# A state-space mixer's head: the second normalisation on ScalarE, and another order of the first step

## The chip, the cores and the metric

The kernel runs on one core of a Trainium2 chip. The metric is the device time of one execution in microseconds, the median of several runs. TensorE multiplies, VectorE, ScalarE and GpSimd compute element by element, SyncE (SP) issues most of the transfers; ScalarE's instruction stream issues some too. Each engine runs its own list of instructions strictly in order, and the engines wait for one another through counted semaphores.

## What is computed

Input x is 2 sequences of 2048 tokens with 256 features, float32. A conditioning vector c gives six modulation rows per sequence. Then:

```python
h = _layernorm(x) * (1 + ca) + sa
xn = _layernorm(h, ln_w, ln_b)          # the second normalisation
xz = xn @ W_in.T                        # xp and z, 512 channels each
xc = silu(conv1d(xp, 4 taps) + b_conv)
dt, B, C = split(xc @ W_x.T)            # 16 + 16 + 16 rows
dt = softplus(dt @ W_dt.T + b_dt)
h_t = h_{t-1} * exp(dt_t * A) + dt_t * u_t * B_t    # 16 states a channel
y = ((h_t . C_t) + xc * D) * silu(z)
# forward and backward over time, then x + ga * (h + 0.5 * (y_fwd + y_bwd) @ W_out.T)
# then a second modulated normalisation and a mixture of 8 experts, 2 taken per token, and a shared one
```

## The kernel before

The tokens are 8 blocks of 512. The kernel has a head, a scan stage and an expert stage; the change touches the head and the first units of the scan stage.

**The scan stage** has 16 steps q (block and direction alternating, even q forward). A step has 16 units T, four to each chunk c of 128 channels. A unit has 4 parts i. For a unit VectorE multiplies the step input by the B rows (`multiply`, L1350; every fourth unit GpSimd does it, L798), ScalarE computes four decays exp(dt*A) into the PSUM banks 0 to 3 (`decay`, L1102), VectorE scans the four parts (`scan`, L1364), GpSimd multiplies by the C rows (`weigh`, L810), and TensorE adds up the states of four units (`sum_chunk`, L1760 and L1764). A decay of part i waits until the part's previous scan has read the bank (`scan_done`), so ScalarE can be at most one unit ahead. TensorE brings 32 channels of the step input to all partitions (`spread_input(U)`, L1752); it needs VectorE's multiply two units earlier to be done, as there is one bank.

While a step is scanned, the engines prepare the next one in fixed slots (T mod 16, n): projections of xp (`project_x`, L1689), convolution as 4 tap matmuls (`convolve`, L1708), their copies by ScalarE (`copy_xp`, L1011 to 1018, `copy_conv`, L1045), silu (L1052), the 48 rows of B, C and dt (`project_xdbl`, L1731, `copy_x_dbl`, L1059), `project_dt` (L1740) and softplus in three passes (L1071, L1073, L1076) and a log (L1082). GpSimd adds the two parts of softplus (`add_dt`, L785) and multiplies dt by xc (`step_input`, L790). All of these share two PSUM banks in one fixed sequence (`bank_uses`). In the T loop ScalarE's slots CONV_AT are (2,1), (2,2), (5,1), (6,0): `copy_conv(q+1, 0)` comes after decay (2,1).

**Transfers of a step.** SP runs one list. `spread_rows(q)` stores the B and C rows and loads them to all partitions, 8 transfers of 256 KB (L577). `store_dt` (L585) writes a chunk's dt to DRAM, `spread_dt` (L594) reads it back broadcast (4 x 256 KB) for the decays, `spread_dtu` (L603, L608) does so with dt*xc for GpSimd's multiply. Everything SP issues goes into one queue.

**The head** prepares all 8 blocks in the order of ORDER. For each block n VectorE takes statistics of x (L1278, L1281, L1284), modulates (L1293, L1299) to H, takes statistics of H, and one block later normalises (`normalise`, L1310) into one of three buffers xn. GpSimd computes the reciprocal roots (`power`, L761) and, ahead of that, the diagonal tap matrices of both directions (L771, 8 instructions), which SP stores in DRAM and loads again where they are needed. TensorE turns a block (`turn_block`, L1665), ScalarE copies it with ln_w and ln_b applied (`copy_turned`, L980) and issues two stores (`keep_block`): H to t_scratch and the turned block to xnT_scratch, 512 KB each. Blocks 0 and 1 are also the first two steps' inputs. The first step's own preparation is woven between the blocks by hand, on TensorE and on ScalarE. At its end stand the last block's copy, behind decay (0,3), and before it the scaling of w_out (L1130). SBUF of the head lies under the buffers dbu and hst of the scan stage, so before the first multiply VectorE waits for the taps to be stored and for mod_scratch (`taps_kept`, `mod_stored`; SP issues the latter at L630, behind spread_dt(0, 0)), and before unit 2's scans for all H and xnT stores. The order of the blocks between the steps, and two of the waits:

```python
copy_block(3)
copy_x_dbl(0)
softplus(0, 0)
softplus_log(0, 0)
for c in range(1, NC):
    softplus(0, c)
softplus_log(0, 1)
copy_block(4)
...
dve.wait_ge(taps_kept, 32)
dve.wait_ge(mod_stored, 16)
multiply(0)
```

## Time and profile before

| | |
|---|---|
| median of 3 runs | 2238.55 us (2237.41 to 2240.18) |
| the profiled execution, its own time | 2238.26 us |
| its span in the profile | 2236.5 us |
| busy: PE, PEld, DVE, ACT, POOL | 83%, 34%, 92%, 60%, 81% |
| granted TensorE clock, mean | 0.874 |
| DMA, mean | 116 GB/s |

Times in rows are microseconds from the start of the span unless marked otherwise. PE is TensorE, PEld its weight loads, DVE VectorE, ACT ScalarE, POOL GpSimd; SPq and ACTq are the instructions by which those engines issue transfers. In a line of the timeline the first number is the start, the second the duration of the merged group, and a bracket tells how long the engine was idle before it and what ended that. A float32 matmul is recorded as two instructions. The clock column is a share of 2.4 GHz.

### The profile page before, as it was taken

To read this page: it belongs to the slowest core of one execution; us is meant where nothing else is said; L and a number is where in the kernel's file an instruction comes from. 1 tells how busy PE (TensorE), PEld (TensorE's weight loads), DVE (VectorE), ACT (ScalarE), POOL (GpSimd) and SP (SyncE) were. 2 spreads that over 40 slices of the span, in tenths; PEclk is the share of its full clock that TensorE was granted. 3 is DMA by queue.
4 is the path that set the end of the run, shared out by engine and by line. 5 is a ranking of instruction groups with operands and counts; after the bars stand their busy time and mean duration, and the time that the engine had idled before them with its cause. 6 is when DMAs were issued, how large, how long until landed. Compare 5 with 4: busy or idle time off the path is not lost.

```text
span 2236.5 us, 24275 instructions
## 1 busy us (share of the span) xinstructions
PE 1847.3 (83%) x6152; PEld 765.3 (34%) x6153; DVE 2047.3 (92%) x2381; ACT 1342.3 (60%) x2404; POOL 1811.6 (81%) x652
## 2 busy tenths in 40 slices
PE   7687887878797879788787878797956699999997
PEld 3222332323232323233232323231312366655554
DVE  7899999999999999999999999999999877557776
ACT  3566757585766757675758576666755343424443
POOL 3389999999999999999999999999999434325444
PEclk9777988989898979798898989797967799999999
DMA  7734434343434344353534353444434462235554
GB/s 285 227 89 106 121 102 123 96 112 106 113 106 112 107 115 115 100 121 101 125 94 115 103 120 105 105 109 119 96 89 134 161 237 102 83 86 83 79 80 67
DMA packets 136494, 259.95 MB, mean 116 GB/s; under 512 B 19984, under 2 KB 42768, under 8 KB 135232
## 3 DMA queue, kind: packets, MB, share of 16 engines
q1 hardware_dynamic: 120064, 230.78, 38.8%
q0 software_dynamic: 13440, 17.93, 4.8%
q10 hardware_dynamic: 2880, 9.96, 1.1%
q8 instruction: 46, 0.75, 0.1%
q14 instruction: 64, 0.52, 0.1%
HBM read 190.32 MB, written 69.34 MB: 116 GB/s over the span
## 4 chain that ended last, share of the span: by engine, by line
DVE 47%; PE 22%; issue 14%; POOL 5%; ACT 4%; DMA 3%; DVEq 3%; SPq 1%; POOLq 0%; ACTq 0%
DVE hst L1364 30%; DVE dbu L1350 9%; PE psum L1764 4%; PE psum L1889 4%; POOL hst L810 3%; PE psum L1708 3%; PE psum L1722 2%; PE psum L1901 2%; PE psum L1752 2%; DVEq L1598 1%; DVE h L1608 1%; PE psum L1689 1%; DVE h L1620 1%; DMA b_rep<-bc_scratch 1%; ACT psum L1102 1%
## 5 line engine op out<-in xcount | busy, mean ns | idle before, releaser
L810 POOL TENSOR_TENSOR hst<-hst,c_rep 128x2048 f32<-128x2048 f32 x255 | 1152.1, 4536 | 22.6 <-ACT state L1090 20.1
L1102 ACT ACTIVATE psum<-dt_rep,neg_a 128x512 f32<-128x512 f32 x1024 | 692.8, 684 | 442.8 <-DVE hst L1364 433.8
L1364 DVE TENSOR_TENSOR_SCAN hst<-psum,state,dbu 128x512 f32<-128x512 f32 x768 | 919.3, 1257 | 0.0
L1350 DVE TENSOR_TENSOR dbu<-psum,b_rep 128x2048 f32<-128x2048 f32 x192 | 434.8, 2265 | 17.3 <-PE psum L1752 12.8
L1752 PE MATMUL psum<-dt,same 32*128 32x512 f32 x384 | 253.0, 743 | 192.8 <-DVE dbu L1350 184.5
L1764 PE MATMUL psum<-hst,same 128*32 128x512 f32 x2048 | 311.4, 763 | 50.3 <-POOL hst L810 42.0
L798 POOL TENSOR_TENSOR dbu<-dtu_rep,b_rep 128x2048 f32<-128x2048 f32 x64 | 291.7, 4558 | 45.8 <-DVE hst L1364 45.8
L1364 DVE TENSOR_TENSOR_SCAN hst<-psum,dbu 128x512 f32<-128x512 f32 x256 | 291.1, 1198 | 0.7 <-ACT psum L1102 0.7
L1708 PE MATMUL psum<-xp,taps 128*128 128x512 f32 x512 | 246.6, 632 | 5.6 <-ACTq L1019 4.8
L930 POOL DMA_INDIRECT out_x<-h,target_u x72 | 113.2, 1572 | 156.9 <-DMA out_x<-h,target_u 77.5
L1752 PEld LDWEIGHTS psum<-dt,same 32*128 32x128 f32 x384 | 64.9, 208 | 339.6 <-DVE dbu L1350 255.7
L1764 PEld LDWEIGHTS psum<-hst,same 128*32 128x32 f32 x2048 | 71.9, 136 | 301.7 <-issue 222.3
L1952 PE MATMUL psum<-w,h 128*128 x288 | 145.0, 627 | 8.2 <-issue 2.8
L1708 PEld LDWEIGHTS psum<-xp,taps 128*128 128x128 f32 x512 | 98.8, 200 | 150.8 <-issue 149.7
L1689 PE MATMUL psum<-xnT,w_in 128*128 128x512 f32 x256 | 133.2, 647 | 18.4 <-ACT xc L1045 17.4
L894 POOL DMA_INDIRECT slot_scratch<-send,slot_u x64 | 64.4, 1006 | 102.4 <-ACT send L1202 79.4
L1696 PE MATMUL psum<-xnT,w_in 128*128 128x512 f32 x256 | 127.9, 625 | 11.5 <-ACT sz L1028 11.3
L1760 PE MATMUL psum<-xc,diag_d 128*128 128x512 f32 x128 | 96.0, 841 | 50.0 <-DVE sz L1343 50.0
L1722 PE MATMUL psum<-w_out,sz 128*128 128x256 f32 x512 | 117.0, 382 | 0.0
L1889 PE MATMUL psum<-h2T,sw 128*128 128x512 f32 x256 | 114.8, 602 | 0.4 <-ACT g_silu L1188 0.4
L1722 PEld LDWEIGHTS psum<-w_out,sz 128*128 128x128 f32 x512 | 98.3, 192 | 27.5 <-issue 15.6
L1602 DVE TENSOR_TENSOR h<-psum,b 128x512 f32<-128x512 f32 x72 | 49.8, 691 | 53.8 <-issue 38.4
...
## 6 DMA issues: line engine op xcount, KB each, us to landing
dt_rep<-dt_scratch SPq DMA_DIRECT2D x256, 256.0 KB, 4.7
taps<-taps_scratch SPq DMA_DIRECT2D x64, 256.0 KB, 2.9
b_rep<-bc_scratch SPq DMA_DIRECT2D x64, 256.0 KB, 5.0
c_rep<-bc_scratch SPq DMA_DIRECT2D x64, 256.0 KB, 8.0
dt_scratch<-dt SPq DMA_DIRECT2D x64, 256.0 KB, 2.0
dtu_rep<-dtu_scratch SPq DMA_DIRECT2D x256, 64.0 KB, 1.9
...
```

What stands on the lines that cost most here:

```text
L798: nc.gpsimd.tensor_tensor(dbu[:, U % DBU, :, :], dtu_rep[:].broadcast_to((P, NG, TB)), b_rep[U // UNITS % 2][:], ALU.mult).then_inc(pool_m ...
L810: nc.gpsimd.tensor_tensor(h, h, c_rep[q % 2][:], ALU.mult).then_inc(prod_done, 1)
L1102: nc.scalar.activation(psum[:, PS_A + i, :], dt_rep[:, G % 2, j, :], ACT.Exp, scale=neg_a[:, q % 2, u, i:i + 1]).then_inc(exp_done, 1)
L1350: nc.vector.tensor_tensor(dbu[:, U % DBU, :, :], psum[:, PS_U:PS_U + 1, :].broadcast_to((P, NG, TB)), b_rep[U // UNITS % 2][:], ALU.mult). ...
L1364: nc.vector.tensor_tensor_scan(time_order(hst[:, U % RING, i, :], backward), time_order(psum[:, PS_A + i, :], backward), time_order(dbu[:, ...
L1689: ins = nc.tensor.matmul(psum[:, bank, :], w_in[:, q % 2, k, c * P:(c + 1) * P], xnT[:, q % 2, k, :], start=(k == 0), stop=(k == KD - 1))
L1708: ins = nc.tensor.matmul(psum[:, bank, :], taps[:, c % 2, j, :], xp[:, c % 2, at:at + TB], start=(j == 0), stop=(j == TAPS - 1))
L1722: ins = nc.tensor.matmul(psum[:, bank, half * DM:(half + 1) * DM], sz[:, c, tok], w_out[:, q % 2, c, :], start=False, stop=(half == 1 and ...
L1752: nc.tensor.matmul(psum[:, PS_U, :], same[part, :], dtu[part, c, :], start=True, stop=True).then_inc(u_full, 1)
L1764: ins = nc.tensor.matmul(psum[CH * j:CH * (j + 1), PS_Y, :], same[:, 0:CH], hst[:, (GN * G + j) % RING, i, :], start=False, stop=(i == NG ...
L1889: ins = nc.tensor.matmul(psum[:, bank, :], w[:, k, c * P:(c + 1) * P], h2T[:, j % 2, k, :], start=(k == 0), stop=(k == KD - 1))
L1952: ins = nc.tensor.matmul(psum[:, 2 + r % 2, :], xtT[:, r % 2, k * P:(k + 1) * P], w13[:, bass.ds(e * KD + k, 1), :].rearrange("p a n -> p ...
```

## The change

1. ScalarE normalises (`normalise`, one activation with scale 1/s and bias -m/s per 128 tokens) instead of VectorE; GpSimd computes the bias with two small multiplications a block (`shift`).
2. The taps of the backward direction are built by ScalarE (`late_taps`, 16 activations) after the first two copies of xp; SP stores them just before it needs them.
3. Diagonals (`skip_weights`), the decays' exp and sign (`negate_decays`) and w_out's scaling leave the place before the first block and before the T loop.
4. TensorE does the first step's projections and convolutions in one run after block 0, then block 1, x_dbl, dt 0 and 1, blocks 2 to 4, and the inputs of units 0 to 2 with dt 2 and 3; blocks 5 to 7 come after `convolve(1, 0)`, through one PSUM bank (`LATE = 5`). ScalarE ends softplus 1 to 3 and blocks 5 to 7 in `first_units`, behind decays (0,3) to (2,0).
5. VectorE bounds the gates after all blocks, waits for mod_scratch only at unit 1 and for the rest at unit 3; SP stores mod_scratch after `spread_dtu(0, 0)`. Buffers move so that units 0 to 2 lie over memory that is free sooner.

The diff, cut; a line of "..." marks what is left out:

```diff
-d_skip = sb1("d_skip", [P, 2, NC])
...
+pad_to(pre, with_scans + (DBU + 3) * NG * TB * 4)
+d_skip = sb1("d_skip", [P, 2, NC])
...
+minus_one = sb1("minus_one", [P, NT])
+minus_mean = sb1("minus_mean", [P, NBLK * NT])
...
-    return PS_Y if n == LAST else 2 * ((n - 1) % 2) + kd
+    return PS_Y if n >= LATE else 2 * ((n - 1) % 2) + kd
...
     sp.wait_ge(taps_built, NC)
-    for D in range(2):
-        sp.wait_ge(taps_built, NC * (D + 1))
-        sp.dma_start(taps_dram[NC * D:NC * (D + 1)].rearrange("k p n -> p k n"),
-                     taps_out[:, NC * D:NC * (D + 1)].rearrange("p k t m -> p k (t m)")).then_inc(taps_kept, 16)
+    sp.dma_start(taps_dram[0:NC].rearrange("k p n -> p k n"),
+                 taps_out[:, 0:NC].rearrange("p k t m -> p k (t m)")).then_inc(taps_kept[0], 16)
     sp.dma_start(w_in[:, 1], A["w_in"][:, 1]).then_inc(w_late, 16)
     sp.dma_start(w_out[:], A["w_out"]).then_inc(w_late, 16)
-    sp.wait_ge(taps_kept, 32)
+    sp.wait_ge(taps_kept[0], 16)
...
     for k in range(6):
+        if k == NC:
+            sp.wait_ge(late_taps_built, NC * TAPS)
+            sp.dma_start(taps_dram[NC:2 * NC].rearrange("k p n -> p k n"),
+                         taps_out[:, NC:2 * NC].rearrange("p k t m -> p k (t m)")).then_inc(taps_kept[1], 16)
+            sp.wait_ge(taps_kept[1], 16)
         load_taps(*divmod(k, NC))
...
     spread_dt(0, 0)
+    spread_dtu(0, 0)
     sp.wait_ge(mod_step, 8)
     sp.dma_start(mod_dram, mod[:, :, 2:6, :]).then_inc(mod_stored, 16)
-    spread_dtu(0, 0)
     store_dt(0, 1)
...
+    def shift(n):
+        part = slice(ORDER[n] * NT, (ORDER[n] + 1) * NT)
+        pool.wait_ge(p1_rstd, 2 * n + 2)
+        nc.gpsimd.tensor_tensor(minus_mean[:, part], mv[:, 1, part, 0], rstd[:, 1, part], ALU.mult
+                                ).then_inc(p1_shift, 1)
+        pool.wait_ge(p1_shift, 2 * n + 1)
+        nc.gpsimd.tensor_tensor(minus_mean[:, part], minus_mean[:, part], minus_one[:], ALU.mult
+                                ).then_inc(p1_shift, 1)
...
-    pool.wait_ge(half_set, 1)
+    pool.wait_ge(half_set, 2)
...
-    for D in range(2):
-        if D == 1:
-            power(0, 0)
-        for c in range(NC):
-            nc.gpsimd.tensor_tensor(
-                taps_out[:, NC * D + c], ident[:].rearrange("p (a m) -> p a m", a=1).broadcast_to((P, TAPS, P)),
-                w_conv[:, D, c, :].rearrange("p (t a) -> p t a", a=1).broadcast_to((P, TAPS, P)),
-                ALU.mult).then_inc(taps_built, 1)
-    power(0, 1)
-    for n in range(1, LAST):
+    for c in range(NC):
+        nc.gpsimd.tensor_tensor(
+            taps_out[:, c], ident[:].rearrange("p (a m) -> p a m", a=1).broadcast_to((P, TAPS, P)),
+            w_conv[:, 0, c, :].rearrange("p (t a) -> p t a", a=1).broadcast_to((P, TAPS, P)),
+            ALU.mult).then_inc(taps_built, 1)
+    for n in range(LAST):
...
+        shift(n)
...
+    power(LAST, 0)
     add_dt(0, 0)
-    power(LAST, 0)
+    power(LAST, 1)
+    shift(LAST)
     step_input(0, 0)
-    power(LAST, 1)
     add_dt(0, 1)
...
-    act.wait_ge(w_loaded, 16 * 5)
-    nc.scalar.activation(neg_a[:], neg_a[:], ACT.Exp).then_inc(neg_a_done, 1)
-    act.wait_ge(consts, 2)
-    for D in range(2):
+    for b in range(BATCH):
+        copy_mod(b, 0, (0, 1))
+    copy_mod(0, 1, (None,))
+    copy_mod(0, 2, (1, 0))
+    copy_mod(1, 1, (None,))
+    copy_mod(1, 2, (1, 0))
+    def normalise(n):
+        k = ORDER[n]
+        act.wait_ge(h_done, NT * (n + 1))
+        act.wait_ge(p1_shift, 2 * n + 2)
+        if n >= 3:
+            act.wait_ge(xnT_full, KD * (n - 2))
+        for tt in range(NT):
+            tile = k * NT + tt
+            nc.scalar.activation(xn[:, n % 3, tt, :], H[:, tile, :], ACT.Identity, scale=rstd[:, 1, tile:tile + 1],
+                                 bias=minus_mean[:, tile:tile + 1]).then_inc(p1_norm, 1)
+    def late_taps():
+        act.wait_ge(consts, 2)
+        act.wait_ge(conv_loaded, 32)
...
-            nc.scalar.activation(diag_d[:, D, c, :], ident[:], ACT.Copy, scale=d_skip[:, D, c:c + 1]
-                                 ).then_inc(diag_done, 1)
-    act.wait_ge(neg_a_done, 1)
-    nc.scalar.activation(neg_a[:], neg_a[:], ACT.Copy, scale=-1.0).then_inc(neg_a_done, 1)
+            for tap in range(TAPS):
+                nc.scalar.activation(taps_out[:, NC + c, tap, :], ident[:], ACT.Copy,
+                                     scale=w_conv[:, 1, c, tap:tap + 1]).then_inc(late_taps_built, 1)
+    def skip_weights():
+        for D in range(2):
+            for c in range(NC):
+                nc.scalar.activation(diag_d[:, D, c, :], ident[:], ACT.Copy, scale=d_skip[:, D, c:c + 1]
+                                     ).then_inc(diag_done, 1)
+    def negate_decays():
+        act.wait_ge(w_loaded, 16 * 5)
+        nc.scalar.activation(neg_a[:], neg_a[:], ACT.Exp).then_inc(neg_a_done, 1)
+        act.wait_ge(neg_a_done, 1)
+        nc.scalar.activation(neg_a[:], neg_a[:], ACT.Copy, scale=-1.0).then_inc(neg_a_done, 1)
+    normalise(0)
...
-    def copy_block(n):
+    def turn_copies(n):
...
+    def copy_block(n):
+        turn_copies(n)
...
     act.wait_ge(zeroed, 1)
-    copy_block(0)
+    turn_copies(0)
     for c in range(2):
         copy_xp(0, c)
-    for c in range(2):
-        copy_conv(0, c)
-    copy_block(1)
+    keep_block(0)
+    late_taps()
+    copy_conv(0, 0)
+    normalise(1)
+    copy_conv(0, 1)
     for c in range(2, NC):
         copy_xp(0, c)
-    copy_block(2)
-    for c in range(2, NC):
-        copy_conv(0, c)
+    normalise(2)
+    copy_conv(0, 2)
+    normalise(3)
+    copy_conv(0, 3)
     silu_xc(0)
-    copy_block(3)
+    copy_block(1)
+    normalise(4)
     copy_x_dbl(0)
...
     softplus_log(0, 0)
-    for c in range(1, NC):
-        softplus(0, c)
-    softplus_log(0, 1)
-    copy_block(4)
-    for c in range(2):
-        copy_xp(1, c)
-    copy_block(5)
-    act.wait_ge(w_late, 32)
-    nc.scalar.activation(w_out[:], w_out[:], ACT.Copy, scale=0.5).then_inc(w_out_done, 1)
-    copy_block(6)
+    for n in range(2, LATE):
+        copy_block(n)
+    normalise(5)
+    negate_decays()
     act.wait_ge(neg_a_done, 2)
+    def first_units(T, n):
+        if (T, n) == (0, 3):
+            softplus(0, 1)
+            softplus(0, 2)
+        if (T, n) == (1, 0):
+            softplus(0, 3)
+            softplus_log(0, 1)
+        if (T, n) == (1, 1):
+            copy_xp(1, 0)
+            copy_xp(1, 1)
+        if (T, n) == (1, 2):
+            copy_block(5)
+            normalise(6)
+        if (T, n) == (1, 3):
+            copy_block(6)
+            normalise(LAST)
+        if (T, n) == (2, 0):
+            copy_block(LAST)
+        if (T, n) == (2, 1):
+            skip_weights()
+        if (T, n) == (4, 1):
+            act.wait_ge(w_late, 32)
+            nc.scalar.activation(w_out[:], w_out[:], ACT.Copy, scale=0.5).then_inc(w_out_done, 1)
...
             decay(T, n)
-            if T == 0 and n == 3:
-                copy_block(LAST)
+            first_units(T, n)
             if q > 0 and (t, n) in OUT_AT:
...
-        if n > 0:
-            normalise(n - 1)
...
-        if n == 3:
-            bound_gates()
-    normalise(LAST)
+    bound_gates()
...
-    dve.wait_ge(taps_kept, 32)
-    dve.wait_ge(mod_stored, 16)
+    for D in range(2):
+        dve.wait_ge(taps_kept[D], 16)
     multiply(0)
...
             multiply(T + 1)
-        if T == 2:
+        if T == 1:
+            dve.wait_ge(mod_stored, 16)
+        if T == 3:
+            dve.wait_ge(diag_done, 2 * NC)
             dve.wait_ge(h_stored, 16 * NBLK)
...
                 pe.wait_ge(mod_copied, 10)
-            elif n == LAST:
+            elif n > LATE or (n == LATE and kd > 0):
                 pe.wait_ge(xnT_copied, KD * n + kd)
-            else:
+            elif n < LATE:
                 pe.wait_ge(xnT_copied, KD * (n - 1))
...
         convolve(0, c)
-    turn_block(1)
     for c in range(2, NC):
         project_x(0, c)
-    turn_block(2)
     for c in range(2, NC):
         convolve(0, c)
-    turn_block(3)
+    turn_block(1)
     pe.wait_ge(w_loaded, 16 * 5)
     project_xdbl(0)
-    for c in range(NC):
+    for c in range(2):
         project_dt(0, c)
-    turn_block(4)
+    for n in range(2, LATE):
+        turn_block(n)
+    pe.wait_ge(same_set, 8)
+    spread_input(0)
+    project_dt(0, 2)
+    spread_input(1)
+    spread_input(2)
+    project_dt(0, 3)
     for c in range(2):
         project_x(1, c)
-    turn_block(5)
-    turn_block(6)
-    pe.wait_ge(same_set, 8)
-    spread_input(0)
     convolve(1, 0)
-    turn_xn(LAST, 0)
-    spread_input(1)
-    turn_xn(LAST, 1)
+    for n in range(LATE, NBLK):
+        turn_block(n)
     pe.wait_ge(xnT_copied, KD * NBLK)
-    pe.wait_ge(diag_done, 2 * NC)
-    pe.wait_ge(w_out_done, 1)
...
             sum_chunk(T // GN - 1)
-        if T + 2 < ALL_UNITS and not on_pool(T + 2):
+        if 0 < T < ALL_UNITS - 2 and not on_pool(T + 2):
             spread_input(T + 2)
...
```

## Rows read from the trace of the kernel before

**Rows 1.** Waits of VectorE, 100 to 1720 us: total, times, longest.
```profile
DVE dbu L1350 <- PE psum L1752: 12.8, 9, 2.6
DVE hst L1364 <- ACT psum L1102: 0.7, 1, 0.7
```
**Rows 2.** Windows: length, PE, PEld, DVE, ACT, POOL busy, clock, DMA share, GB/s.
```profile
400.00:500.00 100.00, 81.79 (x271) 29.12 (x270) 100.00 (x78) 68.30 (x118) 95.90 (x28) 0.86 0.45 113
```
**Rows 3.** Timeline of VectorE: the multiplies of units 0, 4 and 8.
```profile
94.25 2.29 DVE L1350 TENSOR_TENSOR dbu<-psum,b_rep 128x2048 f32<-128x2048 f32 x1 [4.22 <-issue]
...
117.39 2.29 DVE L1350 TENSOR_TENSOR dbu<-psum,b_rep 128x2048 f32<-128x2048 f32 x1 [0.52 <-PE psum L1752]
...
145.50 2.29 DVE L1350 TENSOR_TENSOR dbu<-psum,b_rep 128x2048 f32<-128x2048 f32 x1 [2.64 <-PE psum L1752]
```
**Rows 4.** Timeline of VectorE: one block's normalisation.
```profile
24.45 1.38 DVE L1310 TENSOR_SCALAR xn<-H,mv,rstd 128x256 f32<-128x256 f32 x4
```
**Rows 5.** Line 1299 as a whole (ns, min/median/max), and GpSimd's timeline beside its first four.
```profile
L1299 DVE SCALAR_TENSOR_TENSOR H<-H,rstd,mod x32: 466/476/1269, 15.8 to 84.1; 128x256 f32<-128x256 f32 x32
...
15.71 4.57 POOL L771 TENSOR_TENSOR taps_out<-ident,w_conv 128x512 f32<-128x512 f32 x4
```
**Rows 6.** Timeline of ScalarE.
```profile
24.08 2.43 ACT L964 ACTIVATE diag_d<-ident,d_skip 128x128 f32<-128x128 f32 x8
...
55.33 1.28 ACT L1052 ACT_TABLE_LOAD   x1
...
59.85 1.45 ACT L980 ACTIVATE xnT_out<-psum,ln_b,ln_w 128x512 f32<-128x512 f32 x2
...
80.67 1.91 ACT L1130 ACTIVATE w_out<-w_out 128x2048 f32<-128x2048 f32 x1 [0.40 <-ACT xnT_out L980]
...
91.97 2.52 ACT L1102 ACTIVATE psum<-dt_rep,neg_a 128x512 f32<-128x512 f32 x4 [8.06 <-DMA dt_rep<-dt_scratch]
...
110.85 0.67 ACT L1045 ACTIVATE xc<-psum,b_conv 128x512 f32<-128x512 f32 x1
```
**Rows 7.** Windows, columns as in rows 2 (68.23 to 73.80: three softplus on ScalarE).
```profile
72.00:74.00 2.00, 2.00 (x9) 1.63 (x8) 2.00 (x6) 1.94 (x4) 0.55 (x1) 0.50 1.07 220
80.00:82.00 2.00, 0.58 (x5) 0.58 (x6) 2.00 (x7) 1.60 (x2) 1.30 (x2) 1.00 1.03 407
...
111.00:118.00 7.00, 6.43 (x7) 2.18 (x8) 6.48 (x7) 5.33 (x12) 7.00 (x2) 0.50 0.07 21
68.23:73.80 5.57, 4.27 (x11) 2.59 (x12) 5.43 (x24) 5.45 (x10) 2.26 (x2) 0.54 0.97 223
```
**Rows 8.** Timeline of SP's issues.
```profile
66.19 1.75 SPq L577 DMA_DIRECT2D b_rep<-bc_scratch  x4
67.98 1.93 SPq L577 DMA_DIRECT2D c_rep<-bc_scratch  x4
...
85.85 0.90 SPq L630 DMA_DIRECT2D mod_scratch<-mod  x1
```
**Rows 9.** DMA: last c_rep and mod_scratch (us to landing), queues q1 (SP) and q10 (ScalarE), 86 to 88.
```profile
c_rep<-bc_scratch SPq DMA_DIRECT2D x1, 256.0 KB, 9.1
...
mod_scratch<-mod SPq DMA_DIRECT2D x1, 1024.0 KB, 8.3
...
q1 hardware_dynamic: 165, 0.28, 61.3%
q10 hardware_dynamic: 57, 0.23, 34.1%
```
**Rows 10.** Timeline of TensorE.
```profile
47.49 7.04 PE L1708 MATMUL psum<-xp,taps 128*128 128x512 f32 x16
...
93.68 0.60 PE L1665 MATMUL psum<-ident,xn 128*128 128x128 f32 x4
...
99.17 5.40 PE L1708 MATMUL psum<-xp,taps 128*128 128x512 f32 x8 [0.87 <-ACT xnT_out L980]
104.50 1.12 PE L1752 MATMUL psum<-dt,same 32*128 32x512 f32 x2
```

22 lines of the change are left out of this document (10 added, 12 removed).

## The prediction, made before the changed kernel was run

> **What bounds the kernel now.** First ask where a microsecond taken from the head would go. In the long scan stage VectorE hardly waits: its waits over some 1,600 us sum to 13.5 us [rows 1], and a stretch of 100 us shows it busy throughout [rows 2]. So a shift of VectorE's work at about 150 us passes to the end almost whole, and the case is decided between 22 us and the multiply of unit 4. Times below are from the span's start; the profiled execution took 2238.26 us, beside a median of 2238.55, so a shift can be added to either.
>
> Before, the first multiply starts at 94.25, the multiply of unit 4 at 117.39 and that of unit 8 at 145.50 [rows 3]. In front of the first, VectorE had ended its head 4.22 us earlier. What came last was mod_scratch, issued by SP at 85.85 with 8.3 us to landing, thus 94.2 [rows 8, 9]: a transfer at the end of a full queue, not an engine.
>
> **VectorE's head.** Line 1310 goes: 32 instructions, 1.38 us for four with the ends overlapped, about 1.3 net, so 8 x 1.3 = 10.4 us [rows 4]. GpSimd no longer builds the second half of the taps beside the first block: its four multiplies stood at 15.71 to 20.28, and line 1299, normally 0.48 us, took up to 1.27 there, at most 4 x 0.8 = 3.2 us [rows 5]. VectorE is done at 90.0 - 10.4 - 3.2 = 76.4 at the latest; nothing below needs it sooner. By SBUF — State Buffer of the Trainium skill (Who interferes with whom) a VectorE instruction with two SBUF inputs and a GpSimd instruction that reads SBUF exclude each other; by that rule the trace's 1.27 beside 0.48 is what goes. GpSimd gains 17 tiny instructions. Their price isn't in the trace: between nothing and the 1.14 us (4.57/4) of a multiply of 512 columns [rows 5], where these have 4. At the dear end, two of them per block would hold VectorE about a microsecond in each, 8 in all, still covered by the DMA wait below. Cost nil.
>
> **ScalarE up to the first silu.** Before turning block 0 it drops the exp table load, the two decay operations and 8 diagonals, and does normalise(0) from 22.6. One such instruction has 256 elements and two pointer operands: between 0.30 (128 elements, 2.43/8) and 0.72 (512 elements, 1.45/2) [rows 6], by the straight line 0.44, so four are 1.75 and end at 24.3. VectorE's ended at 25.8: 1.5 us won. Late taps are 16 x 0.30 = 4.9 us of ScalarE; they end near 40.7 and hold the copy of the first convolution, about 2 us later than before, but turn_block(1) and (2) are no longer between TensorE's projections and convolutions (1.0 each) and the rest catches up: the fourth conv copy ends near 53.0 instead of 55.3. The silu table is still in from the first silu, so the 1.28 us load at 55.33 falls away, and the silu (1.9 by w_out's row of the same size) is done near 55.0 instead of 58.5 [rows 6]. All up to x_dbl comes 3.5 us earlier. By ScalarE: Activation LUTs of the Trainium skill (What ACT_TABLE_LOAD costs) a switch costs about 2.66 us with its drain; by that the gain would be 4.9 and the time 2244. No wait stands in the trace between the load and the silu, so I keep 1.28.
>
> **The DMA queue decides the start.** x_dbl 3.5 us earlier puts the b/c row loads at 62.7 instead of 66.19 [rows 8]. These eight are 2.1 MB at 220 GB/s with the engines full [rows 7], 9.7 us; the last landed 9.1 us after its issue near 69.4 [rows 9], 78.5, now 75.0. dt(0,0) used to be stored long after them (add_dt stood behind six blocks of powers). Now softplus(0,0) ends some 2 us behind the first row load (its 1.85 by [rows 7]) and an add of 1.2 follows, so the store is issued near 66.6, into the same SP queue behind the rows. It can't land before 75.7. Beside it the ACT queue now stores blocks 2, 3 and 4 at once. Full-queue work from 65.5: rows 9.7; three blocks, 3.1 MB at 407 GB/s [rows 7], 7.7; dt store 0.7; dt_rep 1.05 MB at 0.28/(2 x 0.613) = 228 GB/s [rows 9], 4.6. Sum 22.7: **dt_rep is in at about 88.4**, against 92.0 [rows 6]. (The same sum for before, with mod: 69 + 25.3 = 94.3, seen 94.2.) With the split seen, 61% to 34% [rows 9], the dt store lands near 80.3, dtu is made by 81.7, and the first multiply runs at 83.9, 10 us earlier than before; the second ends near 90. Bounds for dt_rep: 85.5 if SP's queue goes first, 90.5 if the queues alternate evenly.
>
> mod_scratch now follows dtu_rep: issued near 91, landed 96 to 98; VectorE wants it at 96.6, and ScalarE holds those scans longer anyhow. Cost nil.
>
> **ScalarE's list in the first units.** It idles from 77 to 88.4 and then has, in strict order, between decays of 0.63 (2.52/4 [rows 6]) that VectorE's scans wait for:
> - four decays 2.5, softplus 1 and 2 at 1.85 (5.57/3 [rows 7]) 3.7, decay, softplus 3, its log 1.5, decay, two xp copies (estimate from the 0.72 copy plus small ones) 1.7, decay: 13.
> - block 5 must wait for TensorE: xp(1,0) is ready at +11.5, convolve(1,0) comes first in TensorE's order, then a turn: 5.4 + 0.6 [rows 10] = +17.5 (3.5 at full clock, 7 at half).
> - blocks 5, 6, 7 each: copy 0.75, wait for the second half in the one bank PS_Y 0.65, copy 0.75, issue 0.4 (the gap before w_out [rows 6]); normalise(6) and (7) 1.65 each; turns for the next; four decays. Together about 12.7: +30.2.
> - eight diagonals 2.4, copy_conv(1,0) 0.6: **+33.3**, at 121.7.
>
> Before, decays began at 91.97 and that conv copy started at 110.85 [rows 6]: 19 us. So 14 us of list replace 3.5 us of earlier start. The scans show it: (1,3) may run 8 us after (1,2) allows, (2,0) 4, (2,1) 2, (2,2) 2.5.
>
> TensorE goes on once block 7 is copied, 117.7: convolve(1,1) 5.4, then project_x(1,2) 2.8 (1.8 or 3.5 by clock, from 7.04/16 = 0.44 each at full clock; at 0.50 seven took 6.4 [rows 7, 10]), spread_input(4) 1.6 (1.12 [rows 10] or twice): unit 4's multiply at about 127.5, **10 us late**.
>
> Given back: from unit 4 to 8 VectorE idled 3.4 us, 0.7 for ScalarE and 2.64 for spread_input(8), behind convolutions on TensorE [rows 1, 3]. TensorE would arrive there warmed by steady work, so I take 3. Moved w_out scaling, 1.9 [rows 6], is in unit 4 where decays are a unit ahead: nil. Its cover is that lead. Net +10 - 3 = **+7 us: 2245.5**.
>
> **Rivals.** (a) *The head was VectorE's, and the start is what counts.* Perfetto Trace Analysis of the Trainium skill (Optimizing Scalar/DVE Operations) says that offloading to ScalarE may make sense where VectorE is saturated. As a mechanism here: the first multiply comes 10.4 us earlier, ScalarE's list fits beside the scans, and all of it arrives: 2228. For it speaks that the removed work is VectorE's own; against it that its end was 4.2 us before the first multiply, and the list: units 0 to 2 took VectorE 23.1 us with all waits [rows 3], and ScalarE now needs over 30. It decides only if ScalarE's extras shrink by 10 us. Chance 0.13, all of "faster". (b) *Both ends cancel.* SP's queue first (dt_rep 85.5), convolutions at full clock (list +31), unit 4 at 120, 3 given back: -0.5, 2238; up to +4.5. Chance 0.22. (c) *TensorE cold throughout*, at 0.50 as in 111 to 118 [rows 7], even alternation, nothing given back: 90.5 + 37, convolve 7, projection and spread 5.6: unit 4 at 137, 2256 or more. Chance 0.1. (d) *The load or the normalisation isn't what I think* (the table load stays): 1.3 later start, 2247, within the forecast. The forecast itself 0.55.
>
> **Numbers.** A measurement here tells some 0.2%, 4.5 us, from nothing. Slower by more: 0.55 + 0.1 = 0.65; same 0.22; faster 0.13. The range takes in (b) and most of (c): 2236 to 2254 leaves out (a) and the tail of (c), about 2 in 10.
>
> **What would show it.** Right: no L1052 table load before the first silu; dt_scratch landing 10 us or more after issue; first decay 86 to 90, first multiply 82 to 86; gaps of VectorE in units 1 and 2 put down to ScalarE's decays, 10 us or more in all; copy_conv(1,0) over 30 us after the first decay; unit 4's multiply after 120. Wrong: dt_scratch landing in 3 to 4 us, blocks 5 to 7 copied without VectorE waiting, unit 4's multiply before 113.

## The result, and the profile after

The change makes the kernel slower, by a little: 2247.31 us median of 14 runs (2243.89 to 2250.66) beside 2238.76 us of 14 runs of the kernel before (2235.28 to 2242.36). The ratio is 1.0039, its 95% interval 1.003 to 1.0047. The profiled execution has a span of 2245.9 us at a granted clock of 0.875, against 2236.5 us at 0.874. The forecast was 2245.5.

The page's first part says what moved between the engines: VectorE lost 13.6 us of work (from 2047.3), ScalarE gained 17.9 (from 1342.3).

```profile
span 2245.9 us, 24305 instructions
PE 1841.6 (82%) x6152; PEld 762.9 (34%) x6153; DVE 2033.7 (91%) x2349; ACT 1360.2 (61%) x2450; POOL 1809.3 (81%) x665
```

Read VectorE's timeline next, beside [rows 3]. The first number is the start, the brackets at the end hold the idle time before the instruction and what ended it. L1416 is the multiply (L1350 before), L1430 the scan.

```profile
83.16 2.29 DVE L1416 TENSOR_TENSOR dbu<-psum,b_rep 128x2048 f32<-128x2048 f32 x1 [8.44 <-PE psum L1823]
...
107.39 1.22 DVE L1430 TENSOR_TENSOR_SCAN hst<-psum,dbu 128x512 f32<-128x512 f32 x1 [6.77 <-ACT psum L1160]
113.88 1.22 DVE L1430 TENSOR_TENSOR_SCAN hst<-psum,dbu 128x512 f32<-128x512 f32 x1 [5.27 <-ACT psum L1160]
118.30 1.22 DVE L1430 TENSOR_TENSOR_SCAN hst<-psum,dbu 128x512 f32<-128x512 f32 x1 [3.19 <-ACT psum L1160]
121.81 1.22 DVE L1430 TENSOR_TENSOR_SCAN hst<-psum,dbu 128x512 f32<-128x512 f32 x1 [2.29 <-ACT psum L1160]
...
125.29 2.29 DVE L1416 TENSOR_TENSOR dbu<-psum,b_rep 128x2048 f32<-128x2048 f32 x1
...
153.12 2.29 DVE L1416 TENSOR_TENSOR dbu<-psum,b_rep 128x2048 f32<-128x2048 f32 x1 [2.64 <-PE psum L1823]
```

The first multiply starts 11.1 us earlier than before (83.16 against 94.25), that of unit 4 is 7.9 us later (125.29 against 117.39), that of unit 8 is 7.6 us later (153.12 against 145.50). In between, scans wait for decays. The waits of VectorE from 90 to 200 us sum this up; the first fence is the kernel after, the second the kernel before:

```profile
DVE hst L1430 <- ACT psum L1160: 19.5, 7, 6.8
DVE dbu L1416 <- PE psum L1823: 2.6, 1, 2.6
```
```profile
DVE dbu L1350 <- PE psum L1752: 5.5, 4, 2.6
DVE dbu L1350 <- issue: 4.2, 1, 4.2
DVE hst L1364 <- ACT psum L1102: 0.7, 1, 0.7
```

So 11 us won at the start are lost behind it, and 8 more. ScalarE's timeline shows what stands between those decays (L1160 is the decay, L1035 a block's copy, L996 the normalisation, L1012 the diagonals, L1103 the copy of a convolution):

```profile
86.09 2.52 ACT L1160 ACTIVATE psum<-dt_rep,neg_a 128x512 f32<-128x512 f32 x4 [7.99 <-DMA dt_rep<-dt_scratch]
...
98.69 0.67 ACT L1160 ACTIVATE psum<-dt_rep,neg_a 128x512 f32<-128x512 f32 x1
101.82 0.78 ACT L1035 ACTIVATE xnT_out<-psum,ln_b,ln_w 128x512 f32<-128x512 f32 x1 [2.46 <-PE psum L1734]
103.34 0.78 ACT L1035 ACTIVATE xnT_out<-psum,ln_b,ln_w 128x512 f32<-128x512 f32 x1 [0.75 <-PE psum L1734]
...
104.60 2.07 ACT L996 ACTIVATE xn<-H,minus_mean,rstd 128x256 f32<-128x256 f32 x4 [0.49 <-ACT xnT_out L1035]
...
106.68 0.67 ACT L1160 ACTIVATE psum<-dt_rep,neg_a 128x512 f32<-128x512 f32 x1
...
118.20 2.43 ACT L1012 ACTIVATE diag_d<-ident,d_skip 128x128 f32<-128x128 f32 x8
120.53 0.67 ACT L1103 ACTIVATE xc<-psum,b_conv 128x512 f32<-128x512 f32 x1
```

Between the decay at 98.69 and the one at 106.68, ScalarE waits 2.46 and 0.75 us for TensorE's turns, copies, waits 0.49 for its own copy and normalises: eight microseconds in which VectorE has one scan's worth of work (1.22 us). From the first decay to the start of copy_conv(1,0) the list took 34.4 us (86.09 to 120.53), against 18.9 before [rows 6].

In front of the first decay stands SP's queue (a row is an issue, with its line in SP's list; dt_rep reads dt_scratch and is issued when that has landed):

```profile
62.56 1.96 SPq L583 DMA_DIRECT2D b_rep<-bc_scratch  x4
64.56 3.26 SPq L583 DMA_DIRECT2D c_rep<-bc_scratch  x4
67.87 0.69 SPq L591 DMA_DIRECT2D dt_scratch<-dt  x1
79.43 1.86 SPq L600 DMA_DIRECT2D dt_rep<-dt_scratch  x4
...
87.95 0.65 SPq L642 DMA_DIRECT2D mod_scratch<-mod  x1
```

dt(0,0), 256 KB, was issued at 67.87 and had landed when dt_rep was issued at 79.43: 11.5 us.

### The profile page after: what moved, and what is told of

Same layout as the page of the kernel before. It is cut to its first block, busy times and chain, and to the rows that moved or that the text cites. A ratio compares the mean times of both kernels' runs of the same rounds, so it can differ in the third digit from the quotient of the medians.

```text
span 2245.9 us, 24305 instructions
## 1 busy us (share of the span) xinstructions
PE 1841.6 (82%) x6152; PEld 762.9 (34%) x6153; DVE 2033.7 (91%) x2349; ACT 1360.2 (61%) x2450; POOL 1809.3 (81%) x665
## 4 chain that ended last, share of the span: by engine, by line
DVE 43%; PE 26%; issue 13%; ACT 6%; POOL 4%; DMA 4%; DVEq 2%; SPq 1%; POOLq 0%; ACTq 0%; PEldq 0%
DVE hst L1430 30%; DVE dbu L1416 9%; PE psum L1960 4%; PE psum L1837 4%; PE psum L1777 3%; POOL hst L829 3%; PE psum L1793 2%; DMA b_rep<-bc_scratch 2%; PE psum L1972 2%; PE psum L1823 2%; PE psum L2023 2%; PE psum L1758 2%; ACT psum L1160 1%; DVEq L1667 1%; DVE h L1677 1%
## 5 line engine op out<-in xcount | busy, mean ns | idle before, releaser
L1160 ACT ACTIVATE psum<-dt_rep,neg_a 128x512 f32<-128x512 f32 x1024 | 693.1, 684 | 436.3 <-DVE hst L1430 427.1
L1430 DVE TENSOR_TENSOR_SCAN hst<-psum,state,dbu 128x512 f32<-128x512 f32 x768 | 919.6, 1259 | 0.0
L1416 DVE TENSOR_TENSOR dbu<-psum,b_rep 128x2048 f32<-128x2048 f32 x192 | 435.0, 2266 | 20.8 <-PE psum L1823 20.4
L1430 DVE TENSOR_TENSOR_SCAN hst<-psum,dbu 128x512 f32<-128x512 f32 x256 | 291.8, 1199 | 19.5 <-ACT psum L1160 19.5
L914 POOL DMA_INDIRECT slot_scratch<-send,slot_u x64 | 64.3, 1005 | 102.4 <-ACT send L1283 79.4
L1765 PE MATMUL psum<-xnT,w_in 128*128 128x512 f32 x256 | 127.9, 625 | 11.7 <-ACT sz L1086 11.6
```

Source lines behind the costliest of these rows:

```text
L1160: nc.scalar.activation(psum[:, PS_A + i, :], dt_rep[:, G % 2, j, :], ACT.Exp, scale=neg_a[:, q % 2, u, i:i + 1]).then_inc(exp_done, 1)
L1416: nc.vector.tensor_tensor(dbu[:, U % DBU, :, :], psum[:, PS_U:PS_U + 1, :].broadcast_to((P, NG, TB)), b_rep[U // UNITS % 2][:], ALU.mult). ...
L1430: nc.vector.tensor_tensor_scan(time_order(hst[:, U % RING, i, :], backward), time_order(psum[:, PS_A + i, :], backward), time_order(dbu[:, ...
```

## The experiments

Line numbers in a row are those of the kernel that it is from. "Changed" is the changed kernel. Each kernel was timed beside its own runs of the kernel before, on the same chip (medians 2238.53, 2237.96, 2238.72 and 2237.61 us), and the ratio is to those.

**1. Blocks 5 to 7 before the first decay.**

```diff
-LATE = 5
+LATE = NBLK
     normalise(5)
     negate_decays()
+    copy_block(5)
+    normalise(6)
+    copy_block(6)
+    normalise(LAST)
+    copy_block(LAST)
```

The same `copy_block` and `normalise` lines leave `first_units`, and TensorE turns the blocks among spread_input(0) to (2).

> The changed kernel with one part undone: blocks 5 to 7 are normalised, turned and copied before ScalarE's first decay, in its idle time (77 to 86 us), none between the first units. The list theory (ScalarE's strict list in units 1 and 2 holds the scans): the six waits of VectorE for decays in units 1 and 2, 19 us, shrink to under 3; three more blocks to store (3.1 MB) beside dt_rep put the first decay 2 to 5 us later, 88 to 91; unit 4's multiply at 110 to 115 instead of 125.3; time 10 to 14 us below the changed kernel, 2233 to 2237. Rival, TensorE's low clock in the handshakes is the cause: gains of 2 to 4 us only. Rival, the start is what counts: since the start is later, 2 to 5 us slower than the changed kernel.

Measured: 2235.47 us, ratio 0.9989 (0.998 to 0.9998), 11.8 us below changed. VectorE's and ScalarE's timelines:

```profile
82.91 2.29 DVE L1413 TENSOR_TENSOR dbu<-psum,b_rep 128x2048 f32<-128x2048 f32 x1 [8.11 <-PE psum L1820]
...
93.73 4.57 DVE L1427 TENSOR_TENSOR_SCAN hst<-psum,dbu 128x512 f32<-128x512 f32 x4 [3.62 <-ACT psum L1160]
...
114.35 2.29 DVE L1413 TENSOR_TENSOR dbu<-psum,b_rep 128x2048 f32<-128x2048 f32 x1
```
```profile
74.36 0.78 ACT L1035 ACTIVATE xnT_out<-psum,ln_b,ln_w 128x512 f32<-128x512 f32 x1 [6.83 <-DMA xnT_scratch<-xnT_out]
...
92.93 2.52 ACT L1160 ACTIVATE psum<-dt_rep,neg_a 128x512 f32<-128x512 f32 x4 [0.94 <-ACT xnT_out L1035]
```

The first decay comes 6.8 us *later* than in changed (92.93 against 86.09), and unit 4's multiply 10.9 us *earlier*. With the first multiply where it was (82.91 against 83.16), this is the experiment that parts "the start" from "the list": what stands between the decays costs what the change loses. Two sizes in the expectation were off: the first decay came later than 88 to 91, and VectorE still waits 8.5 us for decays, 3.6 of them before the first scan, not under 3. The edit takes the blocks out of ScalarE's list and their turns out from between TensorE's convolutions at once; experiments 2 and 4 touch ScalarE alone.

**2. The diagonals before the first decay, nothing else.**

```diff
     normalise(5)
+    skip_weights()
     negate_decays()
...
-    if (T, n) == (2, 1):
-        skip_weights()
```

> The changed kernel, but the 8 diagonals (2.4 us of ScalarE) are made before the first decay, in idle time, instead of in unit 2. If ScalarE's list alone sets unit 4's multiply, as my sum had it: 2.4 us less. If TensorE's convolve(1,1), which begins only when block 7 is copied, ends last there (in the profile it ended at 122.5 and project_x(1,2) began at once, while the conv copy had been done at 121.1): under 0.5 us less, unit 4's multiply stays at 125.

Measured: 2247.99 us, ratio 1.0038 (1.0024 to 1.0051): nothing won. Unit 4's multiply was at 126.55, 1.3 us later than in changed. A scan before it still waits: its decay stands behind copy_conv(1,1), and that convolution stands on TensorE behind block 7's copy, which hasn't moved:

```profile
125.18 1.22 DVE L1429 TENSOR_TENSOR_SCAN hst<-psum,dbu 128x512 f32<-128x512 f32 x1 [4.26 <-ACT psum L1160]
```

So 2.4 us of ScalarE's work behind block 7 are free. The path runs over the blocks and TensorE, not over the sum of ScalarE's work. The 1.3 us are TensorE's: `convolve(1,1)` started at 117.44 (117.22 in changed) and took 6.31 us instead of 5.26, at a mean granted clock of 0.57 (117.4 to 123.6) instead of 0.69 (117.2 to 122.4).

**3. The C rows behind the dt path.**

```diff
-spread_rows(0)
+spread_rows(0, (0,))           # B rows alone
 store_dt(0, 0)
 ...
 sp.dma_start(mod_dram, mod[:, :, 2:6, :]).then_inc(mod_stored, 16)
+load_rows(0, (1,))             # C rows
```

> The changed kernel, but in the first step SP issues the four loads of the C rows after the dt store, dt_rep, dtu and mod_scratch, instead of ahead of them. Queue theory (the dt store waits in SP's queue behind the rows): dt_scratch lands 3 to 5 us after its issue instead of 11.5, at about 71; first multiply at 76 instead of 83.2; first decay at about 78.3, when ScalarE is free, instead of 86.1; the list behind it is unchanged, so unit 4's multiply comes 7 to 8 us earlier, 117.5, and the time is 2239 to 2241. Rival, the ACT queue's block stores are what delays it: dt_scratch still takes 8 us or more and the gain is under 3 us.

Measured: 2245.72 us, ratio 1.0034 (1.0021 to 1.0046). dt_scratch was issued at 66.80 and had landed at 74.79; first multiply 78.53, first decay 83.44, unit 4's at 123.41. This is the rival's side (8 us to landing, under 3 us won); the 7 to 8 us of the queue theory fell. With no C rows in the queue the store still took 8 us, behind the B rows and beside ScalarE's block stores; experiment 5 tries to part the two.

**4. ScalarE's list made longer by 2.4 us** (the diagonals done twice, once ahead of block 6's copy).

```diff
     if (T, n) == (1, 3):
+        skip_weights()
         copy_block(6)
```

> The changed kernel, but the 8 diagonals are made twice, the first time at (1, 3) ahead of block 6's copy: 2.4 us more in ScalarE's list, nothing else. List theory: every wait behind it moves, unit 4's multiply at 127.7 and the time 2.4 us longer. If the list has slack there: under 0.5 us.

Measured: 2251.92 us, ratio 1.0065 (1.0051 to 1.0079), 4.6 us above changed where 2.4 were expected. The wait of the scan at (2,0) is where it went in: 7.00 us instead of 5.27. Unit 4's multiply is at 128.82, 3.5 us later, for 2.4 us of work.

```profile
116.35 1.22 DVE L1431 TENSOR_TENSOR_SCAN hst<-psum,dbu 128x512 f32<-128x512 f32 x1 [7.00 <-ACT psum L1160]
```

TensorE's timeline has the rest:

```profile
119.69 6.33 PE L1778 MATMUL psum<-xp,taps 128*128 128x512 f32 x8 [0.87 <-ACT xnT_out L1035]
```

`convolve(1,1)` starts 2.5 us later than in changed (117.22). Of these, 0.7 were there before the added diagonals (the last decay ahead of the blocks ran at 99.42 instead of 98.69) and 1.7 came with them, as ScalarE had waited 0.53 us for TensorE at that place. The convolution then takes 6.33 us instead of 5.26, at a mean granted clock of 0.58 instead of 0.69, which is the last 1.1 of the 3.5. The mechanism is the one expected; the 4.6 us hold more than the list's 1.7.

**5. The dt path first** (experiment 3, and ScalarE holds blocks 3 and 4 with their stores until dt(0,0) has landed).

```diff
-for n in range(2, LATE):
+copy_block(2)
+act.wait_ge(dt_stored, 16)
+for n in range(3, LATE):
     copy_block(n)
```

> The changed kernel, C rows later as in the run before, and ScalarE also holds back blocks 3 and 4 (copies and stores) until dt(0,0) is stored. The run with only the C rows later had dt_scratch at 8 us to landing and won 2 us, so the stores of the ACT queue share the blame. Queue theory in full: dt_scratch lands within 4 us, at 71; dt_rep in by 79 to 80, first decay at 79 to 80 instead of 83.4 (C rows later) and 86.1 (changed kernel); unit 4's multiply near 118.5 to 119.5 and the time 2240 to 2242. If dt_scratch still takes 7 us: the load of the B rows alone delays it.

Measured: 2242.53 us, ratio 1.0017 (1.0008 to 1.0026). SP's queue and the waits of VectorE from 74 to 240 us:

```profile
66.81 0.34 SPq L595 DMA_DIRECT2D dt_scratch<-dt  x1
70.91 2.20 SPq L604 DMA_DIRECT2D dt_rep<-dt_scratch  x4
```
```profile
DVE hst L1437 <- ACT psum L1165: 21.0, 8, 6.9
DVE dbu L1423 <- PE psum L1830: 5.2, 3, 2.6
```

The same store now takes 4.1 us instead of 11.5. The held blocks are only a part of that, as in this execution SP also issued the B rows sooner (60.71, in experiment 3 at 63.21). Counted from the issue of the B rows, dt had landed after 16.9 us in changed, after 11.5 to 12.4 in the four kernels that have the C rows later and no stores held (experiments 3, 9, 10 and 11), and after 10.2 here: the C rows are worth 4.5 to 5.4 us, the two held blocks 1.3 to 2.2.

The first decay is at 80.96. The first multiply stands at 76.12, 18 us ahead of the kernel before, and the kernel is still slower than before: the waits for decays are all there (21.0 us beside 19.5 in 90 to 200 us of changed). This speaks plainly against rival (a). It doesn't say that an earlier start is worth nothing: against changed the first decay moved by 5.1 us and unit 4's multiply by 5.3.

**6. The other side: the normalisation alone.** From the kernel *before*: ScalarE normalises, GpSimd shifts, the diagonals and the decays' sign move behind block 6; taps, order and late blocks stay as before.

```diff
-nc.vector.tensor_scalar(xn[...], H[...], mv[...], rstd[...], ALU.subtract, ALU.mult)
+nc.scalar.activation(xn[...], H[...], ACT.Identity, scale=rstd[...], bias=minus_mean[...])
```

> The kernel before with one part of the change alone: ScalarE does the second normalisation (GpSimd its bias), the diagonals and the decays' sign moved to ScalarE's idle time before the first decay to make room; the order of the first step's work, the taps on GpSimd, the blocks before the first units and mod_scratch's place as before. If the loss of the changed kernel comes from its order and the exchange of engines is a gain: VectorE's head ends near 80 instead of 90, GpSimd's add for dt(0,0) near 70 instead of 78.8, then the dt store waits behind the C rows, lands near 80 to 81 instead of 83.5, mod_scratch near 91.5 instead of 94.2; first multiply 2 to 3 us earlier and the time 2235 to 2237. Rival, ScalarE's slower normalisation is the loss: 2 us or more above before.

Measured: 2235.72 us, ratio 0.9987 (0.9978 to 0.9996).

```profile
89.73 2.29 DVE L1373 TENSOR_TENSOR dbu<-psum,b_rep 128x2048 f32<-128x2048 f32 x1 [11.68 <-DMA mod_scratch<-mod]
```

VectorE is free 11.7 us before the first multiply, which waits for mod_scratch, and unit 4's multiply (116.39) moves by 1.0 us only. Taking VectorE's 10 us away was worth some 2 us *and cost nothing*: the loss comes from the rest of the change.

**7. mod_scratch later, in the kernel before.** SP stores it behind `spread_dtu(0, 0)`, VectorE wants it at unit 1.

```diff
-sp.wait_ge(mod_step, 8)
-sp.dma_start(mod_dram, ...)
 spread_dtu(0, 0)
+sp.wait_ge(mod_step, 8)
+sp.dma_start(mod_dram, ...)
...
-dve.wait_ge(mod_stored, 16)
 multiply(0)
...
+                if T == 1:
+                    dve.wait_ge(mod_stored, 16)
```

> The kernel before with one part alone: mod_scratch is stored after dtu, and VectorE waits for it at unit 1 instead of before the first multiply. If mod_scratch's landing at 94.2 set the start: the first multiply at 90.0, when VectorE's head ends, the second at 95.4 (spread_input(1) is behind convolve(1,0) on TensorE until 94.3), the third 2.4 us earlier than before; time 2236, 2 to 3 us under before. Rival, TensorE's order is what counts there: less than 1 us.

Measured: 2234.68 us, ratio 0.9982 (0.9973 to 0.9991): 3.3 us for the place of one store and its wait, more than the 1.5 us by which unit 4's multiply moved (115.92). The first multiply is at 89.96 instead of 94.25, so it was this store that held it before, as the prediction read.

**8. Both 6 and 7.**

> Both parts on the kernel before: ScalarE normalises, and mod_scratch is later. Both theories together: first multiply near 85 to 87, dt_rep in at 88 to 89, scans from 92 instead of 100, with only block 7 between the first units, so unit 4's multiply at 109 to 112 instead of 117.4 and the time 2231 to 2234, below before and below the changed kernel with early blocks (2235.5). If it is not under 2236, what holds is TensorE's order (convolve(1,0), turns), not the start.

Measured: 2236.83 us, ratio 0.9992 (0.9983 to 1.0001): not the sum, and told neither from the two parts nor from the kernel before. The expected 2231 to 2234 fell, with unit 4's multiply at 116.05 instead of 109 to 112. VectorE's timeline, and TensorE's:

```profile
85.63 2.29 DVE L1373 TENSOR_TENSOR dbu<-psum,b_rep 128x2048 f32<-128x2048 f32 x1 [7.64 <-PE psum L1776]
...
104.31 2.29 DVE L1373 TENSOR_TENSOR dbu<-psum,b_rep 128x2048 f32<-128x2048 f32 x1 [3.84 <-PE psum L1776]
```
```profile
96.60 6.62 PE L1732 MATMUL psum<-xp,taps 128*128 128x512 f32 x8 [0.87 <-ACT xnT_out L1001]
103.15 1.12 PE L1776 MATMUL psum<-dt,same 32*128 32x512 f32 x2
110.23 3.78 PE L1713 MATMUL psum<-xnT,w_in 128*128 128x512 f32 x4 [5.96 <-ACT xc L1066]
```

The first multiply is 8.6 us earlier than before, the third (104.31) 1.3 us. The third can't start before TensorE's spread at 103.15, which stands behind convolve(1,1) at 96.60, which stands behind block 7's copy. A start moved forward alone runs into the next fixed point.

**9. Blocks 5 and 6 early, block 7 at (0,3), C rows later.** Experiment 1 leaves the first decay to ScalarE's own work (92.93), so the blocks and the queue were combined. On TensorE block 7 turns behind spread_input(2).

```diff
-LATE = 5
+LATE = NBLK - 1
     negate_decays()
+    copy_block(5)
+    normalise(6)
+    copy_block(6)
+    normalise(LAST)
 ...
     if (T, n) == (0, 3):
+        copy_block(LAST)
         softplus(0, 1)
```

> The changed kernel with the C rows of step 0 behind the dt path (as in the third experiment) and blocks 5 and 6 turned, copied and stored before the first decay, block 7 copied at (0,3) ahead of the softplus there. In the first experiment the first decay began at 92.9 us on ScalarE's own work, not on dt_rep; block 7's two copies (0.78 each) and the wait ahead of them leave that stretch, so it should begin at 90 to 91.5, and VectorE's waits for decays behind it should stay under 9 us in sum (8.5 in the first experiment), since one block's 1.6 us is within what unit 0 leaves ScalarE (6.9 us on VectorE against 2.5 of decays). Theory (the length of ScalarE's list counts, and with it short the start counts as well): unit 4's multiply 1 to 3 us ahead of the 114.35 of the first experiment, 2232 to 2234.5 us. Rival (the order on TensorE, convolve(1, 1) ahead of spread_input(2), sets what follows): unit 4's multiply at 114 to 115.5, 2235 to 2236.5 us.

Measured: 2235.5 us, ratio 0.9988 (0.9979 to 0.9997). The first decay began at 85.58, far earlier than expected (90 to 91.5). Unit 4's multiply stood at 111.99 as the theory had it, but the time is where the rival put it; VectorE's waits for decays were 9.6 us (80 to 200 us), expected under 9.

**10. Experiment 1 with the C rows later.**

> The first experiment (blocks 5 to 7 before the first decay) with the C rows of step 0 behind the dt path as well, so that dt_rep lands some 3 us sooner. Theory (ScalarE's own list, not the landing of dt_rep, begins the first decay there): first decay at 92 to 93 as in the first experiment, unit 4's multiply at 113.5 to 115, 2234.5 to 2236 us, no difference that can be measured from the first experiment. Rival (the landing of dt_rep or the first multiply still counts): 1.5 to 3 us off, 2232 to 2234 us.

Measured: 2232.46 us, ratio 0.9974 (0.9965 to 0.9983). The theory fell and the rival held:

```profile
71.74 0.78 ACT L1040 ACTIVATE xnT_out<-psum,ln_b,ln_w 128x512 f32<-128x512 f32 x1 [5.23 <-DMA xnT_scratch<-xnT_out]
...
89.86 2.52 ACT L1165 ACTIVATE psum<-dt_rep,neg_a 128x512 f32<-128x512 f32 x4 [0.46 <-ACT xnT_out L1040]
```

ScalarE's own work did begin the first decay, but that list stands itself behind a store: block 4's copy waits for block 2's store to leave the buffer, 6.83 us in experiment 1, 5.23 here, and starts at 71.74 instead of 74.36. I had taken "ScalarE's own list" for something that a queue doesn't move. The first decay, unit 4's multiply (111.28) and the median all move by 3.0 to 3.1 us (3.2 with each median set against its own runs of before).

**11. Softplus ahead of block 7's copy.** Three kernels had the same distance from softplus(0,1) to unit 4's multiply (95.40 to 114.35; 93.01 to 111.99; 92.32 to 111.28), so the next bound was taken to be that chain.

```diff
     if (T, n) == (0, 3):
-        copy_block(LAST)
         softplus(0, 1)
         softplus(0, 2)
     if (T, n) == (1, 0):
         softplus(0, 3)
+        copy_turned(LAST, 0)
         softplus_log(0, 1)
+        copy_turned(LAST, 1)
+        keep_block(LAST)
```

On TensorE block 7's turns move between project_x(1,0) and project_x(1,1).

> The sixth experiment (C rows later, blocks 5 and 6 before the first decay) with block 7's copies no longer ahead of softplus(0, 1) but behind softplus(0, 3), in two halves around its log, and block 7's turns between project_x(1, 0) and project_x(1, 1) on TensorE. Theory: with ScalarE's list short, unit 4's multiply is set by a chain that begins at softplus(0, 1), goes over project_dt(0, 3), project_x(1, 0) and (1, 1), both convolutions, project_x(1, 2) and spread_input, and took 18.95, 18.98 and 18.96 us in the first, sixth and seventh experiments (95.40 to 114.35, 93.01 to 111.99, 92.32 to 111.28). Here softplus(0, 1) should start at 88.1, behind the four decays from 85.58, and the turns add 1.2 to 2.5 us to the chain: unit 4's multiply at 108.3 to 109.6, 2229 to 2231 us. Rival (the order of the ScalarE list still holds the scans, or the rest waits on VectorE or on spread_input of unit 8 anyway): unit 4's multiply at 111 to 112, or earlier but with unit 8's still at 139 to 140; 2232 to 2235.5 us.

Measured: 2231.8 us, ratio 0.9972 (0.9962 to 0.9982), between the theory's range and the rival's and 0.2 us from the latter. Unit 4's multiply (112.78) was later than either had it, unit 8's (139.74) where the rival put it. TensorE's timeline, from project_x(1,0) to the convolutions:

```profile
93.31 3.78 PE L1762 MATMUL psum<-xnT,w_in 128*128 128x512 f32 x4
96.88 1.06 PE L1738 MATMUL psum<-ident,xn 128*128 128x128 f32 x4
98.81 1.12 PE L1738 MATMUL psum<-ident,xn 128*128 128x128 f32 x4 [0.87 <-ACT xnT_out L1040]
99.72 3.39 PE L1762 MATMUL psum<-xnT,w_in 128*128 128x512 f32 x4
102.94 7.03 PE L1781 MATMUL psum<-xp,taps 128*128 128x512 f32 x16
```

Softplus(0,1) started at 90.02, not 88.1: block 4's copy waited 5.46 us for block 2's store (4.11 in experiment 9) and the first decay began at 87.57. The chain grew from 18.96 to 22.76 us. From the first projection to the convolutions it took 9.63 us (93.31 to 102.94), in experiment 10 5.78 (95.62 to 101.40): the turns that I moved in are 2.2 us with 0.87 for ScalarE's copy between the halves, and the projections around them ran slower. Experiments 10 and 11 can't be told apart in time. Both are faster than the kernel before and than the change.

Where the shift of unit 8's multiply (from 145.50) went in the medians, over all kernels:

| kernel | first multiply | unit 4 | unit 8 | shift of unit 8 | median to before |
|---|---|---|---|---|---|
| before | 94.25 | 117.39 | 145.50 | | |
| changed | 83.16 | 125.29 | 153.12 | +7.6 | +8.6 |
| 1 blocks 5 to 7 early | 82.91 | 114.35 | 142.28 | -3.2 | -3.1 |
| 2 diagonals early | 82.93 | 126.55 | 154.91 | +9.4 | +9.5 |
| 3 C rows later | 78.53 | 123.41 | 151.66 | +6.2 | +7.2 |
| 4 list longer | 83.38 | 128.82 | 157.19 | +11.7 | +13.4 |
| 5 dt first | 76.12 | 119.98 | 147.76 | +2.3 | +4.6 |
| 6 normalisation alone | 89.73 | 116.39 | 143.36 | -2.1 | -2.2 |
| 7 mod later | 89.96 | 115.92 | 144.32 | -1.2 | -3.3 |
| 8 both | 85.63 | 116.05 | 142.97 | -2.5 | -1.1 |
| 9 block 7 at (0,3) | 79.15 | 111.99 | 139.88 | -5.6 | -3.2 |
| 10 early, C later | 80.00 | 111.28 | 139.41 | -6.1 | -6.3 |
| 11 softplus first | 81.12 | 112.78 | 139.74 | -5.8 | -5.8 |

The last column follows unit 8's shift to within 2.4 us; it doesn't follow the first multiply's. From the first decay to unit 4's multiply it is 39.0 to 42.3 us in the five kernels with blocks 5 to 7 between the decays (39.2 in changed), 26.4 and 25.2 with block 7 alone (experiments 9 and 11), 25.4 in the kernel before, and 21.4 with none (experiments 1 and 10).

The traces also tell where the rest of the last column is. From the start of unit 8's multiply to the start of the scan stage's last, the thirteen profiled executions take 1593.8 to 1595.2 us. From there to the end they take 497.6 to 500.0 us in eleven of them, and 494.3 and 494.6 in experiments 6 and 8, whose profiled executions were 4.2 and 5.4 us under their medians. So the shift reaches the end of the scan stage whole, and what departs from it arises in the last 500 us, in part from one execution to the next.

## Why the prediction was right, and where its terms were off

The forecast was that the start comes some 10 us earlier, ScalarE's list in the first units loses it and more, and 7 us are left. That is what happened, and experiments 1, 4 and 5 show the mechanism from three sides: take the blocks out of the list, make it longer, move the start. How near the number came is in part luck, as the last terms show.

- **VectorE's head.** Line 1380 (1299 before) now takes 1.67 us for its first four; VectorE's last head instruction ended at 74.7 against "76.4 at the latest". GpSimd's tiny instructions took 0.20 us each, near the lower bound. Cost nil holds: VectorE then waited 8.44 us.
- **ScalarE to the first silu.** The table load before it is gone, the silu ended at 54.83 (forecast 55.0). normalise(0) ran from 22.67 to 24.7, 0.49 us each instead of the interpolated 0.44. By ScalarE: Activation LUTs of the Trainium skill (What ACT_TABLE_LOAD costs) an estimate for 256 elements with two pointer operands is 0.585 us, less 0.093 of overlap; the trace agrees, with a median of 0.586 us for one and 2.06 for four.
- **The DMA queue.** B and C rows at 62.56 (62.7), store issued 67.87 (66.6), landed 79.4 (80.3), first multiply 83.16 (83.9), dt_rep in at 86.1 (88.4, bounds 85.5 to 90.5). The store came late by 1.3 us; SP took 3.26 us to issue the C rows ahead of it, where it had taken 1.93 before. The split that I had assumed, 61% for SP's queue and 34% for ScalarE's, was the reverse while the C rows and the block stores were both under way: in 70 to 74 us

```profile
q10 hardware_dynamic: 276, 1.02, 63.6%
q1 hardware_dynamic: 329, 0.60, 40.7%
```

  (queue, packets, MB, share; q10 is ScalarE's). The block stores were nearly done by 79 us (q10 moved 0.20 MB in 79 to 86), so dt_rep had the engines almost to itself: 6.7 us from 79.43 to 86.09, where the forecast had 8.1. The store's landing came out within 0.9 us although the split behind it was the wrong way round; that is luck. That ScalarE's stores are the store's other competitor was argued in the prediction and is borne out by experiment 5, at 1.3 to 2.2 us for two blocks; the C rows weigh more.
- **mod_scratch.** Issued at 87.95, 4.4 us to landing, 92.4 instead of 96 to 98. No wait for it: nil holds.
- **ScalarE's list.** 34.4 us to the start of copy_conv(1,0), 32.7 expected (its end at +33.3). Two terms were off against each other. convolve(1,0) took 3.6 us, at full clock, where I took 5.4, and block 5's copy came at +15.7 instead of +17.5. Blocks 5 to 7 took 16.4 us (101.82 to 118.20), where I took 12.7: TensorE idled 3.4 us ahead of the turns of blocks 6 and 7, which then ran at 1.12 us, the lower of its two levels, against the 0.60 of the first; ScalarE waited 1.21 us for a second half instead of 0.65, and had 2.07 us of normalisation instead of 1.65. The 12.7 was also short as a sum: the terms named for it, with four decays, make 13.5 before any turn (in the trace three decays stand there). The stalls were 6.8, 5.3, 3.2 and 2.3 us against 8, 4, 2 and 2.5.
- **TensorE to unit 4.** Block 7 copied 117.2 (117.7), convolve(1,1) 5.26 (5.4), project_x(1,2) 1.88 (2.8) and the spread 1.12 (1.6): the granted clock rose while the convolution ran, 0.69 on average in 117.2 to 122.4 us and 1.00 in 122.4 to 124.2. Unit 4 at 125.29, +7.9 instead of +10.1.
- **Given back.** This step failed: 3 us expected, 0.3 seen. I had argued that TensorE would arrive warmed. It doesn't: it waits for VectorE before the next spread, and starts at the lower level (0.50 in 134.3 to 136.3) as before. The first fence is the kernel after, the second the kernel before:

```profile
134.29 2.07 PE L1823 MATMUL psum<-dt,same 32*128 32x512 f32 x2 [5.53 <-DVE dbu L1416]
136.29 9.40 PE L1777 MATMUL psum<-xp,taps 128*128 128x512 f32 x16
```
```profile
126.39 2.07 PE L1752 MATMUL psum<-dt,same 32*128 32x512 f32 x2 [3.32 <-DVE dbu L1350]
128.39 9.67 PE L1708 MATMUL psum<-xp,taps 128*128 128x512 f32 x16
```

  The two last terms were both mis-sized by 2 to 3 us and cancelled: +7.9 - 0.3 = +7.6 against +10 - 3 = +7. The profiled execution is 9.4 us longer than that of before; the scan stage's last multiply is 7.3 us later (1747.7 against 1740.4), and the other 2 us lie behind it, in a part that the change doesn't touch. Their cause is open.
- **Rival (a)**, that ScalarE's list fits beside the scans and the start alone counts, is refuted for this kernel by experiments 1 and 5. The start is a second term and not nothing: with the list short, 3.1 us of earlier first decay gave 3.0 us (experiment 10), and with the blocks still in it 5.1 us moved unit 4's multiply by 5.3 (experiment 5). Rival (b) would have needed a unit 4 at 120, which is what experiment 5 reached by an earlier start alone. Of (c), the turns of blocks 6 and 7 were slow, and the first two projections mostly (0.61 in 92.0 to 97.7 us); convolve(1,0) and project_x(1,2) ran at full clock.
